# A fused embedding, quantized-attention and expert kernel on one core: V's way back, its rounding, and what stands ahead of three meetings

## The chip, the cores and the metric

The kernel runs on one core of one Trainium2 chip. The metric is the device time of one execution in microseconds (us), as the median of several runs.

## The reference

The reference embeds 64 images (36 patches each) and 64 texts (32 tokens each) to 192 features, gives them one layer of attention whose numbers are quantized, and then a layer of experts. Cut to the attention:

```python
y = x @ fq_weight(w_qkv).T + b_qkv          # x: 64 sequences of 68 rows, 192 wide
y, _ = fq_act(y)                            # scale from min and max over all of y, round to 8 bits
q, k, v = split(y)                          # 12 heads of 16
attn = einsum('bhnd,bhmd->bhnm', q, k) * hd ** -0.5
attn, s_attn = fq_act(attn)                 # scale from min and max over all scores
attn = int_log_softmax(attn, s_attn)        # integer softmax, powers of two
o = einsum('bhnm,bhmd->bhnd', attn, v)
o, _ = fq_act(o)                            # again min and max over everything
o, _ = fq_act(o @ fq_weight(w_proj).T + b_proj)
```

Each `fq_act` needs the extremes of a whole tensor before its first value can be rounded. So the program has stretches, and between them everything meets.

## The kernel before, in words

Every engine has a hand-written instruction stream. Semaphores order them, and `barrier` (L120) is a meeting of all five: each engine drains, counts `all_engines_done` up, and waits for five times the number of the meeting.

**Projections.** A loop over steps `s` makes, in each of 16 of its steps, one unit of Q, K and V. ScalarE moves Q and K from PSUM to SBUF. For V the vector engine (`scale_v`, L1306) scales PSUM into `vst`, which has two buffers by the unit's parity, and SyncE (`store_v`, L591) stores it to `v_rows` in DRAM, in the order sequence position, sequence, feature. `scale_v` of a unit waits (L1309) until the stores of the unit two before it have landed. `load_v` (L603) brings V back with all 68 positions of a run of sequences on 68 partitions: 51 KB a sequence. The list `V_LOADS` (L218) holds step, unit waited for, first and last sequence. All of this is on SyncE's one queue, in program order: in step 26 the loads of sequences 32 to 47 and 0 to 5, then the stores of units 14 and 7, after step 27 those of unit 15, then (L631) the load of 48 to 63.

**First meeting, then the first pass.** For each of 8 chunks `c` of 8 sequences ScalarE adds a magic number to Q and K (`to_halves`, L916), the vector engine rounds and clamps them (`to_whole`, L1390), and GpSimd spreads the last four positions' queries over heads (L753 to L762). SyncE loads sequences to the lower partitions (`load_four`, L640; `load_seqs`, L635), the tensor engine makes scores (`first_scores`), and the vector engine takes their row maxima and minima (`extremes`, L1407). After the last chunk ScalarE adds the magic number to all of V (`vt`, L940), and the vector engine rounds it to `VQ`:

```python
dve.wait_ge(sem("v_added"), 2)
ts(VQ, vt, s1(Q_CAPM, N), H16 + 512.0, ALU.min, ALU.subtract)
```

Then the vector engine reduces the extremes to one column each (L1434 to L1438), GpSimd reduces over the partitions (`reduce_pair`, L731; L764), and the vector engine makes some 45 scalars from the result (L1441 to L1491) and, in L1492 to L1495, constants for the output's bias (`bmask`, `vrow`, `bprow`).

**Second meeting, then the second pass.** It computes the scores again, two sequences a group, 32 groups: loads (`load_two`, L649), scores (`second_scores`, L1997), `distances` on the vector engine (L1505), remainders, logarithms, probabilities and the sum over V. GpSimd clears `stv` first (L774), and SyncE waits for that before its first load. `spread_v` (L655) copies `VQ` to `stv`. In its last step SyncE also issues `load_rest` (L662): the residual rows `hf` and the experts' weights `wsplit`.

**Third meeting**, then the output's extremes over the partitions, the projection of the output, and the experts.

Of the kernel before, what the change touches and what calls it, by code (L numbers as in the profile page):

```python
# [12 lines left out]
ALU = mybir.AluOpType  # L13
# [5 lines left out]
P = 128  # L19
B = 64  # L20
# [70 lines left out]
def program(nc, x, x_txt, tok_W, tok_b, tok_pos, embed, W1, b1, W2, b2, w_qkv, b_qkv, w_proj, b_proj,  # L91
            w_fc_sh, w_proj_sh, w1, w2, router_w, balance_bias, ident_c, headmask_c, select_c, lower_c, out):
    ctx = ExitStack()
    with ctx:
# [24 lines left out]

        def barrier(eng, name):  # L120

            n = barriers.get(name, 0) + 1
            barriers[name] = n
            eng.drain().then_inc(sem("all_engines_done"), 1)
            eng.wait_ge(sem("all_engines_done"), 5 * n)

# [90 lines left out]
        UNIT_ORDER = [UNITS_AT[k] for k in sorted(UNITS_AT)]  # L217
        V_LOADS = [(20, 11, 24, 32), (24, 12, 6, 24), (26, 6, 32, 48), (26, 6, 0, 6), (None, 15, 48, B)]  # L218
        LN_TILES = [(0, 16), (16, 22), (22, 28), (28, 34), (34, 37), (37, 40)]
# [297 lines left out]
        def _(sp):  # L517
# [91 lines left out]
            for s in range(STEPS + 1):  # L609
                if s in (5, 11):  # L610
                    sp.wait_ge(sem("by_patch"), s + 1)
                    load_images(2 + s // 6)
                for at, unit, first, end in V_LOADS:
                    if s == at:
                        if end == 48:
                            for a in range(2):
                                sp.wait_ge(sem(f"w_stored{a}"), 16 * sum(WCH_DMAS[a::2]))
                        if first == 0:
                            sp.wait_ge(sem("h_out"), 16 + 4 * GRID)
                        load_v(first, end, UNIT_ORDER.index(unit) if unit < 15 else 15)  # L620
                if s - 2 in WSTEP:
                    store_split(WSTEP.index(s - 2))
                if s in (7, 13, 19, 25):
                    store_image(s // 6 - 1)
                if s - 1 in UNITS_AT:
                    store_v(UNIT_ORDER.index(UNITS_AT[s - 1]))
            sp.wait_ge(sem("t_stored"), 16 * 16)
            for a in range(2):
                sp.wait_ge(sem(f"h_stored{a}"), 32)
            sp.wait_ge(sem("qkv_extremes"), 16)  # L630
            load_v(48, B, 15)  # L631
            barrier(sp, "sp")


# [13 lines left out]

            def load_two(g, par, half):  # L649
                wait(sp, "scored", 32 + g - 1)  # L650
                load_seqs(par, bass.ds(g * 2, 2), 2)

            pipeline(sp, [(load_four, 0)], 16)
            barrier(sp, "sp")
            def spread_v(g, par, half):  # L655
                wait(sp, "o_summed", g - 1)
                for b in range(2):
                    for a in range(2):
                        sp.dma_start(stv[:, par, b, a].rearrange("p (j h d) -> p j h d", h=2, d=HD)[:, :, a, :],  # L659
                                     VQ[:, bass.ds(g * 2 + b, 1), :].rearrange("p o (j h d) -> p (o j) h d", h=2, d=HD)[:, :, a, :]).then_inc(sem(f"v_spread{par}"), 16)  # L660

            def load_rest(g, par, half):  # L662

                if not (isinstance(g, int) and g == 31):
                    return
                for k in range(2):
# [3 lines left out]

            sp.wait_ge(sem("v_cleared"), 1)
            pipeline(sp, [(load_two, 0), (spread_v, 4), (load_rest, 4)], 32)
            barrier(sp, "sp")

# [43 lines left out]
        def _(pool):  # L718
# [34 lines left out]
            for c in range(8):  # L753
# [8 lines left out]
                last.then_inc(sem("qk_chunk"), 1)  # L762

            reduce_pair(A_MX, "a_minmax")  # L764
            barrier(pool, "pool")
# [38 lines left out]
        def _(act):  # L804
# [127 lines left out]
            for c in range(8):  # L932
                to_halves(c)

            act.wait_ge(sem("qk_whole"), 8)
            act.wait_ge(sem("qk_chunk"), 8)
            act.wait_ge(sem("v_in"), 16 * len(V_LOADS))
            for n in range(2):
# [182 lines left out]
        def _(dve):  # L1121
# [283 lines left out]


            def extremes(c):  # L1407
                for i in range(4):
# [17 lines left out]
            for c in range(9):  # L1426
                if c < 8:
                    to_whole(c)
                if c >= 1:
                    extremes(c - 1)  # L1430
            dve.wait_ge(sem("v_added"), 2)
            ts(VQ, vt, s1(Q_CAPM, N), H16 + 512.0, ALU.min, ALU.subtract)
            dve.wait_ge(sem("extremes"), 32)
# [57 lines left out]
            ch(dve.memset(s1(A_PB), 128.0 * (127.0 + 1.0 + H16) + 64.0))  # L1491
            for k, (lo, hi) in enumerate(((C1, C1 + 3), (C1 + 1, P), (C1 + 2, P))):  # L1492
                ch(dve.tensor_reduce(bmask[:, k:k + 1], ident[:, lo:hi], X, ALU.add, negate=k > 0))
            ch(dve.reciprocal(vrow, prow))
            ch(tt(bprow, bprow, vrow, ALU.mult))  # L1495
            barrier(dve, "dve")
# [345 lines left out]
        def _(pe):  # L1842
# [148 lines left out]
            def first_scores(g, par, half):  # L1991
                pe.wait_ge(sem(f"st_qk{par}"), (half + 1) * 48)
                for k in range(2):
                    wait(pe, "extremes", g * 2 + k - 1)
                    scores(g * 2 + k, 4 * k, par, 2 * k, 2)

            def second_scores(g, par, half):  # L1997
                pe.wait_ge(sem(f"st_qk{par}"), (8 + half + 1) * 48)
                wait(pe, "dist", g)
                scores(g, 0, par, 0, 1)  # L2000

            pipeline(pe, [(first_scores, 0)], 16)
            barrier(pe, "pe")

# [218 lines left out]
```

## Time and profile before

| | |
|---|---|
| time, median of 3 runs | 942.96 us (940.64 to 943.77) |
| the profiled execution | 945.13 us, span 943.2 us |
| TensorE's mean granted clock in it | 0.709 of full speed |
| busy: tensor, vector, scalar, GpSimd | 604.6, 709.8, 515.3, 252.1 us |
| HBM read and written | 45.62 and 31.85 MB, 82 GB/s over the span |
| chain that ended last, by engine | vector 28%, tensor 24%, issue 17%, SyncE's queue 16%, scalar 9% |

The profiled execution is one run of its own, 2.2 us above the median. The busy times overlap. The chain is followed back from the last instruction, at each step to what released it; its share by engine says on whom the end hung, and "issue" is time in which nothing recorded was waited for. Where a row names an engine with a q (SPq), it is the engine's queue, issuing.

### The profile page before, as it was taken

Reading aid. Unit: us, or ns where it says so; the run is one execution under the profiler, and the core shown is the slowest. Engines: PE = TensorE matmul, PEld = TensorE weight load, DVE = VectorE, ACT = ScalarE, POOL = GpSimd, SP = SyncE. Lnnn points to the kernel's source line nnn. Section 1 sums busy time; section 2 is a strip of 40 time slices with the busy share of each in tenths; the row PEclk is TensorE's granted clock in tenths of the full one; section 3 lists DMA queues with packets and bytes.
Section 4 is the critical chain, followed back from the end, with each engine's and each line's share of the span. In section 5 each row is a group of like instructions: output and inputs, shape, how many; then the busy total and the mean of one; then the engine's idle time right before and its main releaser. Section 6 shows DMA issues by size and latency. Waiting matters only on the chain.

```text
span 943.2 us, 19819 instructions
## 1 busy us (share of the span) xinstructions
PE 604.6 (64%) x6474; PEld 451.9 (48%) x6474; DVE 709.8 (75%) x1831; ACT 515.3 (55%) x951; POOL 252.1 (27%) x245
## 2 busy tenths in 40 slices
PE   3589889898406667058888888341222349999970
PEld 2589768776204334024555555331112237777760
DVE  2535668777548999789999999987776788667783
ACT  3122268766345424048888888454554226888840
POOL 2022111120011221012222222110355750036575
PEclk9999789999755555555565555555555569999985
DMA  7974024443222221022222222451011241467753
GB/s 172 258 202 120 18 54 131 109 119 120 96 66 82 68 68 51 9 47 33 43 43 43 43 43 37 106 220 59 33 55 58 77 147 51 140 188 218 226 168 113
DMA packets 151481, 92.77 MB, mean 98 GB/s; under 512 B 88828, under 2 KB 143684, under 8 KB 151084
## 3 DMA queue, kind: packets, MB, share of 16 engines
q1 hardware_dynamic: 143560, 72.28, 29.3%
q0 software_dynamic: 7856, 19.68, 7.2%
q8 instruction: 34, 0.56, 0.3%
q14 instruction: 31, 0.25, 0.1%
HBM read 45.62 MB, written 31.85 MB: 82 GB/s over the span
## 4 chain that ended last, share of the span: by engine, by line
DVE 28%; PE 24%; issue 17%; SPq 16%; ACT 9%; DMA 3%; POOL 2%; POOLq 0%; DVEq 0%; ACTq 0%
PE ps L1844 19%; SPq L659 8%; ACT R L806 5%; ACT R L809 3%; DVE M L1413 3%; DVE M L1414 3%; SPq L637 2%; POOL R L799 2%; SPq L636 2%; SPq L638 2%; DVE R L1403 2%; DVE R L1801 1%; PE ps L2018 1%; PE ps L2114 1%; PE ps L1869 1%
## 5 line engine op out<-in xcount | busy, mean ns | idle before, releaser
L1844 PE MATMUL ps<-R 128*128 128x256 f16 (+9 forms) x2064 | 310.2, 303 | 53.0 <-DVE R L1801 16.1
L1844 PEld LDWEIGHTS ps<-R 128*128 128x128 f16 (+5 forms) x2064 | 221.6, 129 | 113.3 <-issue 59.1
L806 ACT ACTIVATE R<-ps 128x768 f16<-128x768 f16 (+7 forms) x257 | 159.8, 649 | 93.5 <-PE ps L2018 18.9
L1844 PE MATMUL ps<-M 32*128 32x68 bf16 (+4 forms) x1196 | 100.6, 242 | 117.5 <-DMA M<-R 67.2
L1844 PEld LDWEIGHTS ps<-M 32*128 32x128 bf16 (+3 forms) x1196 | 64.9, 115 | 168.9 <-issue 66.5
L809 ACT ACTIVATE R<-R,sc 128x512 f16<-128x512 f32 (+7 forms) x107 | 83.6, 838 | 105.6 <-DVE R L1403 40.1
L799 POOL DMA_INDIRECT R<-y_by_tile,M x68 | 66.7, 981 | 98.0 <-DMA y_by_tile<-R 79.4
L771 POOL TENSOR_TENSOR R<-R,M 128x884 f32<-128x884 f32 x32 | 53.2, 1664 | 145.5 <-ACT M L958 145.5
L790 POOL DMA_INDIRECT x_by_expert<-R,M x68 | 67.2, 989 | 60.3 <-DVEq L1707 40.5
L806 ACT ACTIVATE R<-R 128x512 f16<-128x512 f32 (+4 forms) x121 | 64.1, 549 | 35.3 <-DVE R L1801 34.5
L2018 PE MATMUL ps<-ident_b,R 128*68 128x128 bf16 x416 | 53.8, 298 | 25.3 <-ACT R L806 23.9
L1844 PE MATMUL ps<-M,R 128*128 128x8 f16 (+3 forms) x358 | 38.7, 242 | 30.5 <-DVE R L1603 21.9
L2018 PEld LDWEIGHTS ps<-ident_b,R 128*68 128x68 bf16 x416 | 39.6, 160 | 33.0 <-ACT R L806 29.4
L2077 PE MATMUL ps<-ident_f,R 128*128 128x128 f16 x102 | 14.0, 309 | 60.4 <-DVE R L1652 60.4
L1806 DVE TENSOR_TENSOR R<-R 128x256 f16<-128x256 f32 x58 | 24.6, 425 | 36.5 <-ACT R L806 36.5
L1844 PE MATMUL ps<-R,M 68*32 68x4 bf16 (+3 forms) x1680 | 46.7, 208 | 3.7 <-DVE R L1314 2.5
L949 ACT ACTIVATE ps<-ps,sc 128x512 f32<-128x512 f32 x64 | 37.2, 603 | 18.2 <-PE ps L1844 17.2
L1511 DVE SCALAR_TENSOR_TENSOR R<-ps,sc,M 128x544 f16<-128x544 f32 x64 | 42.5, 706 | 6.2 <-PE ps L1844 5.6
L1844 PEld LDWEIGHTS ps<-M,R 128*128 128x128 f16 (+2 forms) x358 | 25.9, 119 | 41.2 <-issue 14.8
L741 POOL COPY R<-R 96x768 f32<-96x768 f32 x24 | 20.5, 863 | 91.0 <-PE ps L1906 91.0
L1413 DVE TENSOR_REDUCE M<-ps 128x8 f32<-128x544 f32 x64 | 41.3, 645 | 4.1 <-PE ps L1844 3.9
L1844 PEld LDWEIGHTS ps<-R,M 68*32 68x32 bf16 (+1 forms) x1680 | 36.2, 111 | 11.9 <-issue 5.0
(293 smaller groups left out, 1050.2 us busy)
## 6 DMA issues: line engine op xcount, KB each, us to landing
R<-x_by_expert SPq DMA_DIRECT2D x41, 192.0 KB, 2.6
y_by_tile<-R SPq DMA_DIRECT2D x41, 192.0 KB, 2.3
R<-in_x_dram SPq DMA_DIRECT2D x12, 576.0 KB, 9.0
M<-R SPq DMA_DIRECT2D x16, 260.0 KB, 2.3
M<-R SPq DMA_DIRECT2D x32, 130.0 KB, 2.0
R<-w_split SPq DMA_DIRECT2D x1, 4032.0 KB, 23.1
R<-h_rows SPq DMA_DIRECT2D x1, 3264.0 KB, 14.3
out_dram<-R SPq DMA_DIRECT2D x17, 192.0 KB
```

What stands on the lines that cost most here:

```text
L659: sp.dma_start(stv[:, par, b, a].rearrange("p (j h d) -> p j h d", h=2, d=HD)[:, :, a, :], VQ[:, bass.ds(g * 2 + b, 1), :].rearrange("p o ...
L771: pool.tensor_tensor(L[par], L[par], S[:, par, 1, :].unsqueeze(2).to_broadcast([P, SLOTS, N]), ALU.subtract).then_inc(sem("relative"), 1)
L790: pool.indirect_dma_start(xg, bass.IndirectOffsetOnAxis(ap=slot[:, n, k:k + 1], axis=0), rows2[:, n, :], None).then_inc(sem("scattered"), 16)
L799: pool.indirect_dma_start(gb[:, i % 4, j, k, :], None, yg[0:TILE * ready, :], bass.IndirectOffsetOnAxis(ap=y_slot[:, 2 * i + j, k:k + 1], ...
L806: return act.activation(out_, in_, ACT.Copy)
L809: return act.activation(out_, in_, ACT.Identity, scale=scale, bias=bias)
L949: act.activation(rem[:, cols], rem[:, cols], ACT.Square, bias=s1(A_BH)).then_inc(sem("sq"), 1)
L1413: dve.tensor_reduce(rowmax[:, g:g + 1, s0:s0 + 2 * k].rearrange("p o (a s) -> p (o a) s", a=2), sv, X, ALU.max)
L1414: last = dve.tensor_reduce(gmin[:, g * 2 + part:g * 2 + part + 1], sv, mybir.AxisListType.XYZ, ALU.min)
L1511: last = dve.scalar_tensor_tensor(D[:, s0:s0 + 2 * k, :].rearrange("p (a s) k -> p a s k", a=2), score_part(0, part), s1(A_NKK), m.unsquee ...
L1844: return pe.matmul(o, a, b, start=start, stop=stop, skip_group_check=True)
L2018: last = pe.transpose(pPT[:, i, :], slots(Pb[par])[:, at, :], ident_b[:, :])
```

## The change

1. The loads of V on SyncE's queue: steps 20 and 24 keep theirs, cut into pieces of 4 and of 6 sequences. The loads of step 26 and the last one go. In their place ScalarE issues ten loads of 2 or 4 sequences (`V_LATE`) after chunks 1 to 6 of the first pass. Before the first meeting SyncE waits until V and the split weights are stored.
2. GpSimd rounds V to `VQ`, after its last chunk and before the all-reduce of the extremes. The first `spread_v` waits for it (`v_whole`).
3. The constants of the output are made between `to_whole(1)` and `extremes(0)`.
4. `barrier` can take work that an engine issues between counting itself in and waiting. At the second meeting SyncE loads the sequences of groups 0 and 1 there, and the tensor engine makes group 0's scores; the loops leave them out. At the third meeting SyncE issues `load_rest` there.

```diff
-        def barrier(eng, name):
+        def barrier(eng, name, ahead=None):
             n = barriers.get(name, 0) + 1
             barriers[name] = n
             eng.drain().then_inc(sem("all_engines_done"), 1)
+            if ahead:
+                ahead()
             eng.wait_ge(sem("all_engines_done"), 5 * n)
...
-        V_LOADS = [(20, 11, 24, 32), (24, 12, 6, 24), (26, 6, 32, 48), (26, 6, 0, 6), (None, 15, 48, B)]
+        V_LOADS = [(20, 11, 24, 28), (20, 11, 28, 32), (24, 12, 6, 12), (24, 12, 12, 18), (24, 12, 18, 24)]
+        V_LATE = [(1, 0, 4), (1, 4, 6), (2, 32, 36), (2, 36, 40), (3, 40, 44), (3, 44, 48), (4, 48, 52), (4, 52, 56), (5, 56, 60), (6, 60, B)]
...
-            sp.wait_ge(sem("qkv_extremes"), 16)
-            load_v(48, B, 15)
+                sp.wait_ge(sem(f"v_saved{a}"), v_stores(16 + a))
+                sp.wait_ge(sem(f"w_stored{a}"), 16 * sum(WCH_DMAS[a::2]))
             barrier(sp, "sp")
...
+            def load_ahead():
+                for g in range(2):
+                    wait(sp, "scored", 32 + g - 1)
+                    load_seqs(g, slice(g * 2, g * 2 + 2), 2)
+
             pipeline(sp, [(load_four, 0)], 16)
-            barrier(sp, "sp")
+            barrier(sp, "sp", load_ahead)
             def spread_v(g, par, half):
+                if isinstance(g, int) and g == 0:
+                    sp.wait_ge(sem("v_whole"), 1)
...
-            pipeline(sp, [(load_two, 0), (spread_v, 4), (load_rest, 4)], 32)
-            barrier(sp, "sp")
+            pipeline(sp, [(load_two, 0), (spread_v, 4)], 32)
+            barrier(sp, "sp", load_rest)
...
+            pool.wait_ge(sem("v_added"), 2)
+            pool.tensor_scalar(VQ, vt, sc[0:N, Q_CAPM:Q_CAPM + 1], H16 + 512.0, ALU.min, ALU.subtract).then_inc(sem("v_whole"), 1)
             reduce_pair(A_MX, "a_minmax")
             barrier(pool, "pool")
...
             for c in range(8):
                 to_halves(c)
+                for at, first, end in V_LATE:
+                    if c == at:
+                        act.dma_start(yv[:, first:end, :], v_dram[:, first:end, :]).then_inc(sem("v_in"), 16)
...
                 if c < 8:
                     to_whole(c)
+                if c == 1:
+                    output_constants()
                 if c >= 1:
                     extremes(c - 1)
-            dve.wait_ge(sem("v_added"), 2)
-            ts(VQ, vt, s1(Q_CAPM, N), H16 + 512.0, ALU.min, ALU.subtract)
             dve.wait_ge(sem("extremes"), 32)
...
+            def scores_ahead():
+                pe.wait_ge(sem("st_qk0"), 9 * 48)
+                pe.wait_ge(sem("extremes"), 31)
+                scores(0, 0, 0, 0, 1)
...
             pipeline(pe, [(first_scores, 0)], 16)
-            barrier(pe, "pe")
+            barrier(pe, "pe", scores_ahead)
```

SyncE's queue in the last steps of the projections, before. L607 is a load of V, L600 and L596 are stores of V for image and text units, L588 stores residual rows:

```order
L596 DMA v_rows<-R 4x32x192 [waits v_scaled]
L596 DMA v_rows<-R 4x32x192
L607 DMA R<-v_rows 68x3072 [waits v_saved0,v_saved1,w_stored1,w_stored0]
L607 DMA R<-v_rows 68x1152 [waits v_saved1,v_saved0,h_out]
L600 DMA v_rows<-R 16x6x192 [waits v_scaled]
L600 DMA v_rows<-R 16x6x192 x2
```

And the same place now:

```order
L599 DMA v_rows<-R 4x32x192 [waits v_scaled]
L599 DMA v_rows<-R 4x32x192
L603 DMA v_rows<-R 16x6x192 [waits v_scaled]
L603 DMA v_rows<-R 16x6x192 x2
L599 DMA v_rows<-R 4x32x192 [waits v_scaled]
```

The two loads between the stores of unit 6 and those of unit 14 are gone from this queue.

GpSimd at the end of the first pass, before. The ISA row with operands is the all-reduce, the one without is a configuration of the engine:

```order
L758 TENSOR_TENSOR R<-R,headmask 64x8x64 [waits scored]
L733 ISA
L733 ISA sc<-sc 128x2 [waits a_minmax]
L774 MEMSET M 68x1536 [waits all_engines_done]
L771 ISA
```

And now:

```order
L763 TENSOR_TENSOR R<-R,headmask 64x8x64 [waits scored]
L770 TENSOR_SCALAR R<-R,sc 68x12288 [waits v_added]
L738 ISA
L738 ISA sc<-sc 128x2 [waits a_minmax]
L781 MEMSET M 68x1536 [waits all_engines_done]
```

The rounding stands between the last product and the configuration, so that both it and the all-reduce come behind it.

## Rows read from the trace of the kernel before

**Rows 1.** The page, first part: engine, busy us, share of span, instructions.
```profile
PE 604.6 (64%) x6474; PEld 451.9 (48%) x6474; DVE 709.8 (75%) x1831; ACT 515.3 (55%) x951; POOL 252.1 (27%) x245
```
**Rows 2.** The waits from 215 to 271 us: total, times, longest.
```profile
DVE R L1314 <- DMA v_rows<-R: 12.5, 1, 12.5
```
**Rows 3.** The timeline of SyncE's queue, from 240 us: start, us, what, issues.
```profile
245.66 0.63 SPq L607 DMA_DIRECT2D R<-v_rows  x2
246.34 1.85 SPq L600 DMA_DIRECT2D v_rows<-R  x3
248.94 8.52 SPq L596 DMA_DIRECT2D v_rows<-R  x2
```
**Rows 4.** Busy time by window: us, PE, PEld, DVE, ACT, POOL, clock, DMA share, GB/s.
```profile
252.00:263.00 11.00, 0.00 (x0) 0.00 (x0) 0.00 (x0) 0.00 (x0) 0.00 (x0) 0.60 0.25 82
```
**Rows 5.** The timeline of vector and tensor engine around the wait.
```profile
250.97 0.28 PE L1844 MATMUL ps<-R 3*96 3x192 bf16 x1
263.80 0.55 DVE L1314 CUSTOM_DVE_ANT_1 R<-ps,M 96x384 f32<-96x384 f32 x1 [12.49 <-DMA v_rows<-R]
```
**Rows 6.** The timeline at the end of the first pass.
```profile
360.83 10.91 ACT L809 ACTIVATE R<-R,sc 68x6144 f16<-68x6144 f32 x2 [19.65 <-DVE R L1403]
...
378.88 3.42 DVE L1432 TENSOR_SCALAR R<-R,sc 68x12288 bf16<-68x12288 f16 x1
...
383.64 0.38 POOL L733 PARTITION_ALL_REDUCE sc<-sc  x1 [23.01 <-DVEq L1438]
```
**Rows 7.** GpSimd's elementwise work: one timeline row, then groups (busy us, mean ns).
```profile
96.59 2.41 POOL L741 COPY R<-R 96x768 f32<-96x768 f32 x3
...
L758 POOL TENSOR_TENSOR R<-R,headmask 64x512 bf16<-64x512 f16 x8 | 8.5, 1058 | 8.2 <-PE ps L1844 7.6
...
L774 POOL MEMSET M<- 68x1536 bf16 x1 | 1.4, 1375 | 12.3 <-DVEq L124 12.3
...
L758 POOL TENSOR_TENSOR R<-R,headmask 128x512 bf16<-128x512 f16 x8 | 11.0, 1381 | 64.4 <-DVE R L1396 53.6 <-issue 10.9
```
**Rows 8.** GpSimd's configurations (ns, first and last start) and what followed two of them.
```profile
L733 POOLq MODIFY_POOL_CONFIG  x4: 1/6/11, 360.8 to 596.9; - x4
...
L758 POOLq MODIFY_POOL_CONFIG  x2: 7/9/11, 270.1 to 270.2; - x2
...
279.40 3.07 POOL L758 TENSOR_TENSOR R<-R,headmask 128x512 bf16<-128x512 f16 x3 [10.88 <-issue]
...
L729 POOLq MODIFY_POOL_CONFIG  x2: 32/32/32, 88.9 to 88.9; - x2
...
96.33 0.38 POOL L729 PARTITION_ALL_REDUCE sc<-sc  x1 [7.55 <-DVEq L1214]
```
**Rows 9.** The timeline of the output's constants, and of the first extremes.
```profile
393.77 0.66 DVE L1493 TENSOR_REDUCE M<-ident 128x1 f32<-128x3 f32 x3
...
395.85 0.36 DVE L1495 TENSOR_TENSOR M<-M 128x192 f32<-128x192 f32 x1
...
287.04 0.72 DVE L1413 TENSOR_REDUCE M<-ps 128x8 f32<-128x544 f32 x1 [3.90 <-PE ps L1844]
```
**Rows 10.** The timeline around the second meeting.
```profile
374.42 1.95 PE L1844 MATMUL ps<-M 32*128 32x68 bf16 x20 [0.29 <-DVE M L1414]
...
398.22 0.11 DVE L1569 MEMSET M<- 128x64 f32 x1
...
402.88 1.33 DVE L1511 SCALAR_TENSOR_TENSOR R<-ps,sc,M 128x544 f16<-128x544 f32 x2 [4.55 <-PE ps L1844]
```
**Rows 11.** The timeline around the third meeting.
```profile
604.93 8.73 SPq L669 DMA_DIRECT2D R<-w_split  x1
...
612.18 0.17 DVE L1577 TENSOR_SCALAR sc<-sc 128x2 f32<-128x2 f32 x1
...
613.97 0.38 POOL L733 PARTITION_ALL_REDUCE sc<-sc  x1 [17.50 <-SPq L124]
```
**Rows 12.** The waits of the tensor engine from 271 to 380 us.
```profile
PE ps L1844 <- DMA M<-R: 35.4, 2, 33.8
```

More of the change, by code:

```diff
@@ L614, in _ @@
                     if s == at:
[L615 to L620, printed above, removed]
+                        load_v(first, end, UNIT_ORDER.index(unit))
                 if s - 2 in WSTEP:
@@ L649, in load_two @@
             def load_two(g, par, half):
+                if isinstance(g, int) and g < 2:
+                    return
                 wait(sp, "scored", 32 + g - 1)
                 load_seqs(par, bass.ds(g * 2, 2), 2)
+            def load_ahead():
+                for g in range(2):
+                    wait(sp, "scored", 32 + g - 1)
+                    load_seqs(g, slice(g * 2, g * 2 + 2), 2)
             pipeline(sp, [(load_four, 0)], 16)
-            barrier(sp, "sp")
+            barrier(sp, "sp", load_ahead)
             def spread_v(g, par, half):
+                if isinstance(g, int) and g == 0:
+                    sp.wait_ge(sem("v_whole"), 1)
                 wait(sp, "o_summed", g - 1)
@@ L660, in spread_v, with load_rest @@
                                      VQ[:, bass.ds(g * 2 + b, 1), :].rearrange("p o (j h d) -> p (o j) h d", h=2, d=HD)[:, :, a, :]).then_inc(sem(f"v_spread{par}"), 16)
-            def load_rest(g, par, half):
-                if not (isinstance(g, int) and g == 31):
-                    return
+            def load_rest():
                 for k in range(2):
@@ L933, in _ @@
                 to_halves(c)
+                for at, first, end in V_LATE:
+                    if c == at:
+                        act.dma_start(yv[:, first:end, :], v_dram[:, first:end, :]).then_inc(sem("v_in"), 16)
             act.wait_ge(sem("qk_whole"), 8)
             act.wait_ge(sem("qk_chunk"), 8)
-            act.wait_ge(sem("v_in"), 16 * len(V_LOADS))
+            act.wait_ge(sem("v_in"), 16 * len(V_LOADS + V_LATE))
             for n in range(2):
@@ L1404, in to_whole, with output_constants @@
                 last.then_inc(sem("qk_whole"), 1)
+            def output_constants():
+                for k, (lo, hi) in enumerate(((C1, C1 + 3), (C1 + 1, P), (C1 + 2, P))):
+                    ch(dve.tensor_reduce(bmask[:, k:k + 1], ident[:, lo:hi], X, ALU.add, negate=k > 0))
+                ch(dve.reciprocal(vrow, prow))
+                ch(tt(bprow, bprow, vrow, ALU.mult))
             def extremes(c):
@@ L1491, in _ @@
             ch(dve.memset(s1(A_PB), 128.0 * (127.0 + 1.0 + H16) + 64.0))
[L1492 to L1495, printed above, removed]
             barrier(dve, "dve")
@@ L1995, in first_scores @@
                     scores(g * 2 + k, 4 * k, par, 2 * k, 2)
+            def scores_ahead():
+                pe.wait_ge(sem("st_qk0"), 9 * 48)
+                pe.wait_ge(sem("extremes"), 31)
+                scores(0, 0, 0, 0, 1)
             def second_scores(g, par, half):
+                if isinstance(g, int) and g == 0:
+                    return
                 pe.wait_ge(sem(f"st_qk{par}"), (8 + half + 1) * 48)
```

## The prediction

> **What bounds the kernel now.** I read the page first: vector engine busy 75% of the span, tensor engine 64%, both far from full [rows 1]. So no engine bounds the whole, and what an edit is worth has to be read at its place. I went to the waits, then to timeline and chain around the three meetings of all engines (`barrier`). They show four stretches in which the chain of waits runs through idle time or side work.
>
> First, the last projections. The vector engine has one wait of 12.5 us for a DMA that writes `v_rows` [rows 2]. SyncE's queue tells why: at 245.66 it issues two loads of V (sequences 32 to 47 and 0 to 5, 1122 KB), at 246.34 the three stores of unit 14, and the next stores take 8.52 us to issue [rows 3]. In between the DMA engines are busy a quarter, at 82 GB/s, and nothing else runs [rows 4]. 1122 KB at 82 GB/s are 14.0 us, so these loads fill the queue until about 260, and the stores behind them land late. `scale_v` of the last unit rewrites their buffer: the vector engine goes on at 263.80 after 12.49 us of idling, since 251.3, and the last matmul of the unit had ended at 251.25 [rows 5].
>
> Second, the end of the first pass. ScalarE adds the magic number to V from 360.83 to 371.74, the vector engine rounds V for 3.42 us from 378.88, and GpSimd's all-reduce, which the scalars wait for, starts at 383.64 [rows 6]. Third, from 393.77 to 396.21 the vector engine makes constants of the output ahead of the second meeting [rows 9], and then idles 4.55 us for the first loads and scores of the second pass [rows 10]. Fourth, at the third meeting everyone waits for SyncE, which needs 8.73 us to issue one load [rows 11].
>
> **The change part by part**, on the profiled execution's clock (945.13 us, 2.2 above the median of 942.96; I carry the difference over to the median).
>
> *V loads off the busy queue: -12.4.* The two loads of step 26 and the one of 48 to 63 leave SyncE; step 20's and step 24's stay, in pieces, the bytes unchanged, in a place where the vector engine shows no wait for a DMA now. So the stores of unit 14 are issued by 248.2 at the head of the queue. Vector engine and tensor engine are both ready at 251.3, so all 12.49 us go unless the stores need more than 3 us to land. Next late would be the last matmul, at no cost. The waits for all saved V, which SyncE now makes before the meeting, replace those that its last load made: nothing.
>
> *Rounding on GpSimd: +8.4 net, the 3.42 us saved on the vector engine included.* The vector engine loses 3.42 us, and its chain to the all-reduce (1.4 us) would be through at about 379.9 + 0.2. But the rounding stands on GpSimd's queue ahead of the all-reduce. It waits for ScalarE's second half, so it starts at 371.8. No row shows this instruction on GpSimd. By the nearest that reads and writes with one input, three copies of 768 elements in 2.41 us, 12288 elements take 12.85 us; the memset of 1536 in 1.375 us gives 11.0; the 512-element products with two inputs give 25.4 us (64 partitions) and 33.1 (128, beside the vector engine's work) [rows 7]. I take the copy, as one input stands nearest: end at 384.6. The Trainium skill, "GPSIMD Engine Reference", § 4.1, calls one-input work on GpSimd roughly line-rate and two-input work about 2x slower than VectorE; its § 3.1 gives 1.03 cycles at 1.2 GHz for a simple body, as an estimate 10.5 us, which would make the sum 2.3 us better.
>
> Then comes what the diff doesn't say. In the order of instructions GpSimd has an ISA row between its last product and the all-reduce, and the trace names it MODIFY_POOL_CONFIG. It ran at 360.8, straight after the last product, and was long over when the all-reduce's data came. The new rounding is ahead of it, so it now runs at 384.6 with the all-reduce waiting behind. Its price: after the pair at 270.1 the first product started at 279.40 after 10.88 us of "issue", 9.2 us behind the config. After the pair at 88.9 the all-reduce could start at 96.33: at most 7.4 us, as it waited for data [rows 8]. For the all-reduce I take 7.4, the row of the same operation; bounds 0 (no row shows a wait in this direction) and 9.2. The all-reduce starts at 392.0 instead of 383.64: +8.4. The Trainium skill, same page, § 2.1, puts the first call after such a config at about 6 us (5.95); with that the sum would be 1.4 us better. The rule speaks against this change, and is my forecast's mechanism rather than a rival's.
>
> *Constants to where the vector engine idles: -2.45.* Their 2.45 us go from 393.77. Their new place is behind `to_whole(1)`, where the engine idled 3.90 us until 287.04 for the first scores [rows 9]. That covers 2.45; without the cover they would cost what they save.
>
> *First loads and scores ahead of the meeting: -4.55.* SyncE's two waits for scores are met when the tensor engine ends its first pass at 376.37; the issue of both groups, six in all, and their landing have until then 10 us and more before the meeting. What stands behind the wait is SyncE's arrival at the meeting, also early enough, and nobody else. The tensor engine scores group 0 while the scalars are made. After the meeting only the clamping of the row maxima remains, over at 398.33 against 402.88 now [rows 10]. The second group's scores wait for the first distances as before. GpSimd's clearing of `stv` only gates loads of group 2.
>
> *SyncE meets before its long load: -1.4.* The vector engine is through at 612.33, the all-reduce runs at 613.97 for SyncE's sake [rows 11]. With 0.2 us of handover it starts at 612.5. The load itself is not issued later.
>
> *Ten loads on ScalarE's queue: +1.0.* ScalarE idles in the first pass, so the issues cost nothing there. But the first two pieces (306 KB, 3.8 us at 82 GB/s) go out at 281, just as the first sequences are loaded, for which the tensor engine has its wait of 33.8 us [rows 12]. Bounds: 0, and 3.8 if the sequences' packets come behind all of them; I take 1, as the tensor engine's loads are already issued in part when the pieces start to move. Behind it the first pass shows one more wait of the tensor engine for a load, 1.6 us, 35.4 less 33.8; the other eight pieces I cost at nothing, on the cover of the vector engine's own work, and each us by which a load came later than that cover would count.
>
> Sum: -12.4 + 8.4 - 2.45 - 4.55 - 1.4 + 1.0 = -11.4. 945.13 gives 933.7; on the median 931.5.
>
> **Rivals.**
> *The config costs nothing where it stands* (chance 0.20). For it: no row shows a reload delaying an all-reduce. Against: the 9.2 us at 270.1 stood on the path. The all-reduce follows the rounding at 384.8: +1.1 instead of +8.4, 924.3; with the memset's rate and no collision of loads 921.4.
> *GpSimd rounds at the pace of its products* (0.24 in three parts). For it: those rows have the same types in and out. Against: two inputs instead of one. The time moves by each us of it. Above 12.85 + 11.4 = 24.3 us (1.98 ns an element) the change is slower than before. At the 64-partition row, 25.4 us: 944.1. At the 128-partition row, 33.1 us: 951.8, the case on the other side. Slower by over 0.3% starts at 2.2 ns an element. Between 1.2 and 1.8 ns: 933 to 940. I give 0.08 to each part.
> *The stores stay late* (0.04): step 24's pieces hold them as those of step 26 did. The rows show no such wait at step 24 now. Then nothing of the 12.4 comes: 943.9.
> The forecast has 0.52.
>
> **How the numbers follow.** A measurement tells about 0.3%, 2.8 us, from no change. Faster: 0.52 + 0.20 + 0.08 = 0.80. Same: the middle part of the pace and late stores, 0.12. Slower: 0.08. The range goes down to the first rival's best, 921.5, and up to 940, the end of the pace still faster; what lies outside holds 0.20.
>
> **What would show it.** The wait for `v_rows` gone and no idle time over 1 us before the last `scale_v`. One GpSimd TENSOR_SCALAR of 68x12288 at 11 to 14 us, then 6 to 9 us of nothing before the all-reduce, both on the chain of waits, and the vector engine idle for some 12 us there. No idle time for `scored` at the start of the second pass. The third all-reduce released by the vector engine, not by SyncE. I would be wrong if the all-reduce followed the rounding within 1 us, if the rounding took over 18 us, or if the vector engine waited for a DMA before 252.

## The result, and the profile after

| | before | after |
|---|---|---|
| time, median | 943.37 us (4 runs, 940.64 to 947.03) | 964.94 us (4 runs, 960.04 to 970.26) |
| ratio, with its 95% interval | 1 | 1.0227 (1.0161 to 1.0293) |
| profiled execution, its span | 945.13, 943.2 us | 966.23, 964.3 us |
| mean granted clock | 0.709 | 0.693 |

The change is slower by 21.6 us; a gain of 11.4 was forecast. The two traces can be laid beside each other at moments that both have. Each line is the time from one moment to the next; the sum is the difference of the spans.

| stretch | before | after | change | forecast |
|---|---|---|---|---|
| start to the first meeting's all-reduce | 268.15 | 254.97 | -13.2 | -12.4 |
| to the first column of the extremes (L1434; now L1450) | 110.73 | 118.37 | +7.6 | +1.0 |
| to the second meeting's all-reduce | 4.76 | 40.71 | +35.9 | +8.4 |
| to the first distances (L1511; now L1523) | 19.24 | 12.24 | -7.0 | -7.0 |
| to the third meeting's all-reduce | 211.09 | 209.73 | -1.4 | -1.4 |
| to the end | 329.2 | 328.3 | -1 | 0 |

(The second line's moment before is the rounding's start of [rows 6], which stood where L1450 now does.) Two forecasts hold to the tenth and the first within 0.8; the two lines far off lie in the first pass and at its end. The lower mean clock asks for no term of its own: the last three lines, over half of the tensor engine's busy time, come out as forecast or 1 us better.

The page, first part and the groups of GpSimd (line, engine, operation, out<-in, count | busy us, mean ns | idle time before and its releaser), of the changed kernel:

```profile
PE 605.6 (63%) x6474; PEld 454.6 (47%) x6474; DVE 704.8 (73%) x1830; ACT 515.1 (53%) x951; POOL 292.2 (30%) x246
...
PE 29%; DVE 28%; issue 15%; ACT 12%; POOL 7%; DMA 6%; SPq 2%; ACTq 1%; DVEq 0%; POOLq 0%
...
L770 POOL TENSOR_SCALAR R<-R,sc 68x12288 bf16<-68x12288 f16 x1 | 41.6, 41647 | 11.2 <-ACT R L816 11.2
```

Against [rows 1], GpSimd is busy 40.1 us more with one instruction more, and the vector engine 5 us less. In the chain that ended last (the second line) SyncE's queue fell from 16% to 2%, while GpSimd rose from 2% to 7% and the DMA engines from 3% to 6%. The engine whose share of busy time is the smallest now bounds a place.

The timeline of the changed kernel at the end of the first pass (start us, us, engine, line, operation, [idle before <-releaser]):

```profile
355.29 10.91 ACT L816 ACTIVATE R<-R,sc 68x6144 f16<-68x6144 f32 x2 [16.70 <-DVE R L1413]
...
366.30 41.65 POOL L770 TENSOR_SCALAR R<-R,sc 68x12288 bf16<-68x12288 f16 x1 [11.21 <-ACT R L816]
...
373.34 0.62 DVE L1450 TENSOR_REDUCE sc<-M 128x1 f32<-128x448 f32 x1
...
414.05 0.37 POOL L738 PARTITION_ALL_REDUCE sc<-sc  x1 [6.10 <-issue]
...
414.45 0.16 DVE L1457 TENSOR_TENSOR sc<-sc 128x1 f32<-128x1 f32 x1 [39.86 <-POOL sc L738]
```

This answers to [rows 6]. The vector engine is through at 374.6 and idles 39.86 us. GpSimd rounds for 41.65 us what the vector engine rounded in 3.42, and the all-reduce comes 6.10 us behind it. The chain of waits over this stretch says the same from the other side, and shows where the 6.10 us lie:

```profile
366.30 41.65 POOL R L770
407.95 0.32 POOLq L124
408.30 5.75 issue
414.05 0.38 POOL sc L738
```

After 0.32 us of the queue's own work come 5.75 us in which GpSimd waits for nothing. GpSimd's configurations in the list of instructions by line (least, middle and longest ns, first and last start) now begin at 408.3, where [rows 8] have 360.8:

```profile
L738 POOLq MODIFY_POOL_CONFIG  x4: 11/11/11, 408.3 to 620.3; - x4
```

The end of the projections, SyncE's queue and the vector engine, answers to [rows 3] and [rows 5]:

```profile
244.24 1.85 SPq L603 DMA_DIRECT2D v_rows<-R  x3
248.35 1.17 SPq L599 DMA_DIRECT2D v_rows<-R  x2
...
250.62 0.54 DVE L1324 CUSTOM_DVE_ANT_1 R<-ps,M 96x384 f32<-96x384 f32 x1
```

No bracket of idle time stands behind the last row: the 12.49 us are gone. The first row is the three stores of unit 14, which that instruction waits for; the two of unit 7 behind them take 1.17 us to issue instead of 8.52.

The first pass is the other surprise. Waits of the changed kernel from 255 to 370 us (total, times, longest), and the tensor engine's timeline there:

```profile
PE ps L1856 <- DMA M<-R: 44.2, 6, 21.8
...
DVE M L1429 <- PE ps L1856: 12.7, 5, 3.7
```

```profile
272.49 3.84 PE L1856 MATMUL ps<-M 32*128 32x68 bf16 x40 [21.82 <-DMA M<-R]
...
287.87 3.85 PE L1856 MATMUL ps<-M 32*128 32x68 bf16 x40 [6.72 <-DMA M<-R]
...
302.78 3.84 PE L1856 MATMUL ps<-M 32*128 32x68 bf16 x40 [6.33 <-DMA M<-R]
...
315.68 3.84 PE L1856 MATMUL ps<-M 32*128 32x68 bf16 x40 [4.32 <-DMA M<-R]
...
328.47 3.84 PE L1856 MATMUL ps<-M 32*128 32x68 bf16 x40 [4.20 <-DMA M<-R]
```

Before, there were two such waits, the first of 33.8 us and one of 1.6 [rows 12]. Now there are six, four of them of 4 to 7 us, and behind five of them the vector engine waits too, 12.7 us in all instead of 3.9. What was late is in the chain of waits: the landings of the sequence loads, one before each of those matmuls.

```profile
267.14 5.21 DMA M<-R
...
279.11 8.61 DMA M<-R
...
294.47 8.17 DMA M<-R
...
309.38 6.16 DMA M<-R
...
322.28 6.05 DMA M<-R
```

In the kernel before the one landing in that chain took 2.00 us. What shares the DMA engines with them is ScalarE's pieces of V. Busy time by window (columns as in [rows 4]) between the sequence loads' issue and landing:

```profile
281.70:287.80 6.10, 0.00 (x0) 0.00 (x0) 4.45 (x10) 0.89 (x2) 1.49 (x1) 0.50 0.43 118
```

The second and third meetings answer to [rows 10] and [rows 11]:

```profile
371.85 1.19 PE L1856 MATMUL ps<-M 32*128 32x68 bf16 x16 [1.01 <-DMA M<-R]
...
628.74 8.72 SPq L674 DMA_DIRECT2D R<-w_split  x1
...
635.57 0.17 DVE L1589 TENSOR_SCALAR sc<-sc 128x2 f32<-128x2 f32 x1
...
636.02 0.37 POOL L738 PARTITION_ALL_REDUCE sc<-sc  x1 [16.16 <-DVEq L124]
```

The scores of the second pass's first group lie in the wait for the second meeting, and the third all-reduce is released by the vector engine 0.28 us after it is through, no longer by SyncE.

### The profile page after: what moved, and what is told of

Its sections match the earlier page's. It is cut to its first block, busy times and chain, and to the rows that moved or that the text cites. A ratio compares the mean times of both kernels' runs of the same rounds, so it can differ in the third digit from the quotient of the medians.

```text
span 964.3 us, 19831 instructions
## 1 busy us (share of the span) xinstructions
PE 605.6 (63%) x6474; PEld 454.6 (47%) x6474; DVE 704.8 (73%) x1830; ACT 515.1 (53%) x951; POOL 292.2 (30%) x246
## 3 DMA queue, kind: packets, MB, share of 16 engines
q10 hardware_dynamic: 720, 1.98, 0.8%
## 4 chain that ended last, share of the span: by engine, by line
PE 29%; DVE 28%; issue 15%; ACT 12%; POOL 7%; DMA 6%; SPq 2%; ACTq 1%; DVEq 0%; POOLq 0%
PE ps L1856 22%; ACT R L813 7%; POOL R L770 4%; DMA M<-R 4%; PE ps L2037 3%; ACT R L816 3%; DMA R<-in_L_txt_tok_embed_dram,R 2%; DVE M L1572 2%; DVE R L1813 2%; POOL R L806 2%; ACT ps L959 1%; DVE R L1523 1%; PE ps L2133 1%; DVE R L1548 1%; DVE M L1553 1%
## 5 line engine op out<-in xcount | busy, mean ns | idle before, releaser
L816 ACT ACTIVATE R<-R,sc 128x512 f16<-128x512 f32 (+7 forms) x107 | 83.6, 838 | 98.8 <-POOL R L763 40.1
L2037 PE MATMUL ps<-ident_b,R 128*68 128x128 bf16 x416 | 55.9, 307 | 24.5 <-ACT R L813 22.8
L2037 PEld LDWEIGHTS ps<-ident_b,R 128*68 128x68 bf16 x416 | 41.5, 166 | 32.2 <-ACT R L813 28.8
L1818 DVE TENSOR_TENSOR R<-R 128x256 f16<-128x256 f32 x58 | 24.6, 424 | 36.7 <-ACT R L813 36.7
L1429 DVE TENSOR_REDUCE M<-ps 128x8 f32<-128x544 f32 x64 | 41.2, 644 | 12.8 <-PE ps L1856 12.7
L770 POOL TENSOR_SCALAR R<-R,sc 68x12288 bf16<-68x12288 f16 x1 | 41.6, 41647 | 11.2 <-ACT R L816 11.2
L763 POOL TENSOR_TENSOR R<-R,headmask 128x512 bf16<-128x512 f16 (+1 forms) x16 | 19.4, 1216 | 80.4 <-DVE R L1406 42.5
```

The source lines that it names most:

```text
L770: pool.tensor_scalar(VQ, vt, sc[0:N, Q_CAPM:Q_CAPM + 1], H16 + 512.0, ALU.min, ALU.subtract).then_inc(sem("v_whole"), 1)
L816: return act.activation(out_, in_, ACT.Identity, scale=scale, bias=bias)
L1429: dve.tensor_reduce(rowmax[:, g:g + 1, s0:s0 + 2 * k].rearrange("p o (a s) -> p (o a) s", a=2), sv, X, ALU.max)
L1818: tt(hl[:, u % 4], hs[:, u % 2, 0], hh[:, u % 4, 0], ALU.subtract)
L2037: last = pe.transpose(pPT[:, i, :], slots(Pb[par])[:, at, :], ident_b[:, :])
```

## The experiments

Two theories had to be told apart at the rounding (its own pace, or what stands around it), two in the first pass (the loads of V, or a drift of the whole stretch), and the three terms that seemed right had to be shown to be right by themselves. Runs are compared with the kernel before on the same chip, and stretches of the traces with each other. The kernel before took 944.37 us beside the runs r5, r6, r7 and r12 and about 1025 us beside the others. In the traces of those others some 80 us more lie behind the third all-reduce (409.7 us in the run of the V loads alone, 329.2 in the kernel before), in the experts, where nothing was changed; of the kernel before itself there is no trace at 1025 us. I take it that ratios and stretches carry over; absolute times don't.

**1. The rounding back on the vector engine** (r1_round_dve), everything else as changed.

```diff
-            pool.wait_ge(sem("v_added"), 2)
-            pool.tensor_scalar(VQ, vt, sc[0:N, Q_CAPM:Q_CAPM + 1], H16 + 512.0, ALU.min, ALU.subtract).then_inc(sem("v_whole"), 1)
...
+            dve.wait_ge(sem("v_added"), 2)
+            ts(VQ, vt, s1(Q_CAPM, N), H16 + 512.0, ALU.min, ALU.subtract).then_inc(sem("v_whole"), 1)
```

> The changed kernel with one part undone: the vector engine rounds V again, 3.42 us behind its last extremes. Theory A (the loss is the rounding's place on GpSimd: 41.65 us of it, then 0.35 + 5.75 us of drain and config, all ahead of the all-reduce): the all-reduce runs at 373.3 + 3.4 + 1.4 + 0.2 = 378.3 instead of 414.05, the time falls by 35.7 us, from 966.2 to about 930.5, and the config is hidden again. Rival B (the collision of V's loads with the first pass, or something behind the second meeting, is most of the loss): it falls by less than 20 us, to 946 or more. In both the first pass keeps its five waits for late sequence loads.

1009.15 us (6 runs), ratio 0.9851 (0.9821 to 0.9881). The all-reduce stood 1 us ahead of where it was expected:

```profile
377.31 0.37 POOL L738 PARTITION_ALL_REDUCE sc<-sc  x1 [23.01 <-DVEq L1454]
```

So the whole change without its rounding on GpSimd is faster than before. The 36.7 us between 377.31 and 414.05 are what the rounding on GpSimd costs. The first pass stays long (118.96 us).

**2. Only the rounding on GpSimd, in the kernel before** (r2_pool_only).

```diff
-            dve.wait_ge(sem("v_added"), 2)
-            ts(VQ, vt, s1(Q_CAPM, N), H16 + 512.0, ALU.min, ALU.subtract)
...
+            pool.wait_ge(sem("v_added"), 2)
+            pool.tensor_scalar(VQ, vt, sc[0:N, Q_CAPM:Q_CAPM + 1], H16 + 512.0, ALU.min, ALU.subtract).then_inc(sem("v_whole"), 1)
             reduce_pair(A_MX, "a_minmax")
```

> The kernel before with that one part alone: GpSimd rounds V, everything else as before. Theory A: the rounding starts at 371.8, takes 41.65 us as in the changed kernel, config 6.1 us, the all-reduce at 419.5 instead of 383.64: 945.1 + 35.9 = 981 us. Rival C (the rounding was slow because of what the change put beside it, the last loads and scores ahead): it takes visibly less here, near the 12.85 us of the prediction, and the time is 950 to 955.

```profile
371.79 41.65 POOL L767 TENSOR_SCALAR R<-R,sc 68x12288 bf16<-68x12288 f16 x1 [11.21 <-ACT R L813]
419.43 0.37 POOL L735 PARTITION_ALL_REDUCE sc<-sc  x1 [5.99 <-issue]
```

One run, 1059.43 us, 34.3 above the median before. By the trace +35.8 (419.43 against 383.64). The same 41.65 us with none of the other edits: what the change put beside it has no part in it.

**3. What the pace hangs on.** Four kernels change only the instruction. r7_copy copies (clamp and subtraction are left out), r6_one_op subtracts only (the clamp is left out), r12_constants has both operations with a constant as the limit of the clamp (the limit is another), r5_half gives GpSimd sequences 0 to 31 and the vector engine the rest.

```diff
-            pool.tensor_scalar(VQ, vt, sc[0:N, Q_CAPM:Q_CAPM + 1], H16 + 512.0, ALU.min, ALU.subtract)
+            pool.tensor_copy(VQ, vt)                                                        # r7_copy
+            pool.tensor_scalar(VQ, vt, H16 + 512.0, None, ALU.subtract)                     # r6_one_op
+            pool.tensor_scalar(VQ, vt, H16 + 640.0, H16 + 512.0, ALU.min, ALU.subtract)     # r12_constants
```

> The changed kernel with GpSimd's rounding of V replaced by a plain copy of the same 12288 elements a partition, f16 to bf16 (clamp and subtraction left out). Theory G (GpSimd's pace hangs on the arithmetic: 3.39 ns an element for two operations, and the copy's pace that the prediction took would have been right for a copy): 12 to 14 us. Theory H (the 16-bit types or the sheer size make it slow): about 40 us.

> The changed kernel with the clamp left out of GpSimd's rounding: one operation, subtract a constant, same data. Theory G: half of the two operations' time or less, 13 to 21 us. Theory I (any TENSOR_SCALAR on GpSimd has this pace, whatever it does): 41.6 us.

> The changed kernel with the clamp's limit as a constant instead of a column of scalars (so V is clamped elsewhere): two operations, no pointer. Theory G: 41.6 us again. Theory J (the pointer operand is what costs): near the one-operation run.

> The changed kernel with sequences 0 to 31 rounded by GpSimd (6144 elements a partition) and 32 to 63 by the vector engine behind its last extremes. If the time goes by elements: 20.8 us on GpSimd, the all-reduce at 366.3 + 20.8 + 6.1 = 393.2 instead of 414.05, the time 20.8 us under the changed kernel's, about 945 on the chip of its profile. If there is a large fixed part: more than 25 us.

The timeline of GpSimd in each, in this order:

```profile
365.36 10.42 POOL L770 CAST R<-R 68x12288 bf16<-68x12288 f16 x1 [11.17 <-ACT R L816]
381.61 0.37 POOL L738 PARTITION_ALL_REDUCE sc<-sc  x1 [5.83 <-issue]
```
```profile
364.97 31.31 POOL L770 TENSOR_SCALAR R<-R 68x12288 bf16<-68x12288 f16 x1 [11.20 <-ACT R L816]
```
```profile
365.52 41.61 POOL L770 TENSOR_SCALAR R<-R 68x12288 bf16<-68x12288 f16 x1 [11.20 <-ACT R L816]
```
```profile
368.06 20.97 POOL L770 TENSOR_SCALAR R<-R,sc 68x6144 bf16<-68x6144 f16 x1 [11.21 <-ACT R L816]
395.01 0.37 POOL L738 PARTITION_ALL_REDUCE sc<-sc  x1 [5.99 <-issue]
```

And the vector engine's half in r5_half:

```profile
375.10 15.54 DVE L1450 TENSOR_SCALAR R<-R,sc 68x6144 bf16<-68x6144 f16 x1
```

| | us | ns an element | one run, us (before: 944.37) |
|---|---|---|---|
| copy | 10.42 | 0.85 | 939.54 |
| one operation | 31.31 | 2.55 | 957.32 |
| two operations, constants | 41.61 | 3.39 | 965.3 |
| two operations, limit from a pointer (as changed) | 41.65 | 3.39 | 966.23 |
| half the elements | 20.97 | 3.41 | 950.45 |

The pace hangs on what the instruction does: from the copy to one operation +1.70 ns, to two another +0.84. The pointer costs nothing, and half the elements cost half. The one-operation run fits neither theory named for it: 31.31 us, against 13 to 21 and against 41.6. The copy took less than the 12 to 14 us expected. A pace like the copy's, on which the forecast rested, is real for a copy, and the copy's run is the forecast's picture: all-reduce at 381.61, 5.83 us behind. Even so that run is only 4.8 us under the kernel before, one run each, where 11.4 had been forecast with a slower copy: its first pass, up to the first column of the extremes, takes 119.76 us instead of 110.73.

The run with half the elements came out at 950.45 us instead of about 945. Its rounding started 1.8 us later than expected, and 2.9 us more lie behind its third all-reduce than in the changed kernel. Its trace shows one thing more. The vector engine's half took 15.54 us, where all of V takes it 3.42 alone: it began at 375.10 beside GpSimd's instruction, which ended at 389.03, and ended 1.6 us after it, and half of 3.42 is 1.71. It looks as if it could hardly move until GpSimd was through; why, no run here isolates. The reductions of float32 from PSUM beside the same instruction kept their 0.57 and 0.71 us. So sharing this rounding between the two engines gains less than the sum of their paces would give.

The Trainium skill, "GPSIMD Engine Reference", § 3.1, has 1.03 cycles an element for a body with a k of at most 2 (read here as the number of operations), at 1.2 GHz as an estimate 10.5 us. The copy agrees; the two operations with one input take four times that. Its § 4.1 calls one-input work roughly line-rate against the vector engine: measured are 3.42 us there and 41.65 here, a factor of 12.

**4. The V loads alone, in the kernel before** (r11_v_only).

```diff
-        V_LOADS = [(20, 11, 24, 32), (24, 12, 6, 24), (26, 6, 32, 48), (26, 6, 0, 6), (None, 15, 48, B)]
+        V_LOADS = [(20, 11, 24, 28), (20, 11, 28, 32), (24, 12, 6, 12), (24, 12, 12, 18), (24, 12, 18, 24)]
+        V_LATE = [(1, 0, 4), (1, 4, 6), (2, 32, 36), (2, 36, 40), (3, 40, 44), (3, 44, 48), (4, 48, 52), (4, 52, 56), (5, 56, 60), (6, 60, B)]
...
                 to_halves(c)
+                for at, first, end in V_LATE:
+                    if c == at:
+                        act.dma_start(yv[:, first:end, :], v_dram[:, first:end, :]).then_inc(sem("v_in"), 16)
```

> The kernel before with the V loads of the change alone (five pieces in steps 20 and 24, ten on ScalarE's queue beside the first pass; rounding, constants and meetings as before). The prediction's -12.4 + 1.0 = -11.4 us against the theory now: the stall of 12.5 us goes, the first pass gives about 7 us of it back in five waits for late sequence loads, net -5 to -6 us, ratio about 0.994.

1018.95 us (12 runs) against 1024.74 (17): ratio 0.9948 (0.9917 to 0.9979), a gain of 5.8 us. The forecast's -12.4 + 1.0 would have been 0.988. The same waits are there as in the changed kernel:

```profile
PE ps L1843 <- DMA M<-R: 44.6, 5, 23.2
...
DVE M L1412 <- PE ps L1843: 16.2, 5, 7.2
```

The all-reduce comes at 379.25, 4.4 us before its old time. The first meeting's comes 13.2 us earlier, and from it to the rounding the first pass takes 119.49 us instead of 110.73: 8.8 us are given back there.

**5. The same late loads, each cut into rows 0 to 63 and 64 to 67** (r3_64_and_4), on top of experiment 1.

```diff
-                        act.dma_start(yv[:, first:end, :], v_dram[:, first:end, :]).then_inc(sem("v_in"), 16)
+                        for rows in (slice(0, 64), slice(64, N)):
+                            act.dma_start(yv[rows, first:end, :], v_dram[rows, first:end, :]).then_inc(sem("v_in"), 16)
```

> As r1_round_dve, and each of the ten late loads of V is cut into rows 0 to 63 and rows 64 to 67; bytes, queue and place unchanged. Theory D (a load of 68 rows runs on 4 of the 16 DMA engines, as the busy share of 0.25 says, and the sequence loads queue behind V on just those four): spread over more engines the pieces are over sooner, the five waits of the tensor engine for a load (6.7, 6.3, 4.3, 4.2, 0.8 us) shrink to under 2 us in all, and the time is 6 to 8 us under r1_round_dve, about 923. Rival E (the collision is one of bytes, or of two queues taking turns): no change, 930.

999.1 us (5 runs, 995.51 to 1000.44), ratio 0.975 (0.972 to 0.9779). The waits from 250 to 366 us, a window in which a piece moves, and the all-reduce:

```profile
PE ps L1857 <- DMA M<-R: 26.8, 5, 18.9
...
DVE M L1428 <- PE ps L1857: 0.5, 1, 0.5
```
```profile
271.00:276.00 5.00, 3.35 (x28) 2.11 (x27) 5.00 (x10) 4.99 (x8) 0.00 (x0) 0.50 0.73 170
```
```profile
363.05 0.38 POOL L738 PARTITION_ALL_REDUCE sc<-sc  x1 [23.01 <-DVEq L1455]
```

The landing of the sequence loads can be read directly. In the DMA issues of the first pass (KB each, median us to landing) the smallest of each three is, in the changed kernel and here:

```profile
M<-R SPq DMA_DIRECT2D x10, 34.0 KB, 6.0
...
M<-R SPq DMA_DIRECT2D x13, 34.0 KB, 2.5
```

The same row of the kernel before has 2.0. The same bytes on the same queue, twice as many loads, and the first pass takes 106.98 us from the all-reduce to the end of the extremes instead of 118.96 in experiment 1. The vector engine's waits fall from 13.3 to 0.5 us. With 68 rows a load of V moved at 82 GB/s with the DMA engines a quarter busy [rows 4]; with 64 rows the window shows 0.73 busy and 170 GB/s, sequence loads included; experiment 6 has a window without them. A quarter of 16 is what the Trainium skill, "DMA: Bandwidth & Descriptors", section "Why a DMA increments its semaphore by 16 and not by 1", would give: the engines used are the largest number up to 16 that divides the slowest dimension on both sides, 4 for 68 rows and 16 for 64. Shares and rates agree; no row here shows which engine carried what. The gain over experiment 1 is 10 us, where 6 to 8 were expected. This is the version to keep: 2.5% below the kernel before.

**6. No late loads in the first pass, but a burst ahead of it** (r8_burst), on top of experiment 1: `V_LATE` is empty, and SyncE issues three loads, each cut at row 64, before the first meeting.

```diff
+            sp.wait_ge(sem("qkv_extremes"), 16)
+            for first, end in ((0, 6), (32, 48), (48, B)):
+                for rows in (slice(0, 64), slice(64, N)):
+                    sp.dma_start(yv[rows, first:end, :], v_dram[rows, first:end, :]).then_inc(sem("v_in"), 16)
             barrier(sp, "sp")
```

> As r1_round_dve, but the late loads of V leave the first pass: SyncE issues them in one burst of three, each in rows 0 to 63 and 64 to 67, after the last unit's extremes and before the first meeting. The first pass then has no V load beside it unless the burst (1938 KB) lasts more than 8 us. Theory D: the first pass has no wait for a late load behind its first, -7.6 us, against a config that takes up to 2.6 us longer beside the loads (9.2 us beside one in the kernel before, 6.6 us without in the changed one): 923 to 926. Rival F (the waits in the first pass come from the shifted start, not from V's loads): they stay, 930 or more.

1007.45 us (5 runs), ratio 0.9818 (0.9786 to 0.9849). That is 1.7 us under experiment 1, within the spread of the two, where 4 to 8 us had been expected. Waits, GpSimd's first product and its configuration, and a window in which the burst alone moves:

```profile
PE ps L1860 <- DMA M<-R: 23.5, 1, 23.5
...
DVE M L1431 <- PE ps L1860: 3.0, 1, 3.0
```
```profile
268.51 3.31 POOL L767 TENSOR_TENSOR R<-R,headmask 128x512 bf16<-128x512 f16 x3 [13.01 <-issue]
...
L767 POOLq MODIFY_POOL_CONFIG  x2: 7/9/11, 257.1 to 257.1; - x2
```
```profile
257.10:262.80 5.70, 0.00 (x0) 0.00 (x0) 1.48 (x7) 4.29 (x8) 0.00 (x0) 0.50 0.97 223
```

Without loads beside it the first pass has one wait of the tensor engine, so the waits of the changed kernel are the late loads' doing and no drift. In the window the DMA engines are 0.97 busy at 223 GB/s, against 0.25 and 82 with 68 rows. But the burst stands beside the configuration ahead of the first product, and from the one to the other it is now 11.4 us (257.1 to 268.5) where the changed kernel has 6.6 (257.0 to 263.63). Up to 2.6 us more had been expected. The extremes' stretch is 113.8 us, between those of experiments 1 and 5. Spreading V in 64-row pieces beats the burst.

**7. The two terms of the second meeting, each undone** on top of experiment 1. r9_no_ahead puts the loads and scores back behind the meeting; r10_const_back puts the constants back behind the scalars.

```diff
-            barrier(sp, "sp", load_ahead)
+            barrier(sp, "sp")
...
-            barrier(pe, "pe", scores_ahead)
+            barrier(pe, "pe")
```
```diff
-                if c == 1:
-                    output_constants()
...
             ch(dve.memset(s1(A_PB), 128.0 * (127.0 + 1.0 + H16) + 64.0))
+            output_constants()
```

> As r1_round_dve, without the loads and scores ahead of the second meeting. The vector engine then idles again for the first scores behind the meeting, 4.5 us, and the time is 4.5 us over that kernel's. If the loads ahead had cost something elsewhere (they stand on SyncE's queue ahead of its wait), less than 4.

> As r1_round_dve, with the constants of the output back between the scalars and the second meeting: from the all-reduce to the first distances 2.45 us more, and the same first pass, as its first scores come late with or without them.

From the all-reduce to the first distances experiment 1 has 12.26 us. Without the work ahead it is 16.56 (+4.30):

```profile
381.48 0.38 POOL L736 PARTITION_ALL_REDUCE sc<-sc  x1 [23.01 <-DVEq L1452]
...
398.04 1.33 DVE L1521 SCALAR_TENSOR_TENSOR R<-ps,sc,M 128x544 f16<-128x544 f32 x2 [4.34 <-PE ps L1854]
```

With the constants back it is 14.72 (+2.46). Both are single runs, 1023.1 and 1018.7 us, and experiment 1's profiled execution took 1014.37. Of the first one's 8.7 us, 4.2 lie ahead of the all-reduce, though its edit comes behind it: its first pass takes 121.75 us up to the rounding, against 118.96 in experiment 1. In the second it takes 122.5, where the same had been expected; whether the constants have a part in that, one run can't tell. Only the stretch behind the all-reduce is evidence.

## Why the prediction was wrong

**The rounding: the term that failed.** "I take the copy, as one input stands nearest" is the step. It put 12.85 us where 41.65 stand, and that alone is 28.8 of the 33 us between forecast and result. The sum with 41.65 in the same place would have been +17.4 instead of -11.4, the right sign and four fifths of the size. The rows had a pointer to it: the products have the same types and do arithmetic, while the copy and the memset do none. The nearest row was sought by the number of inputs; by experiment 3 one operation on one input costs 2.55 ns an element, as much as the products on two (2.1 to 2.7), so in these rows arithmetic makes the difference, and the number of inputs makes little. Even the upper bound, 33.1 us, was 8.5 us short: a product has one operation, and the rounding two. The rival "GpSimd rounds at the pace of its products" had the right sign and half of the mechanism: it took the pace of rows that do arithmetic, but had no term for the second operation. Its worst part (951.8) came nearest, and it was given 0.24 in all. Its condition, slower from 1.98 ns an element, was met at 3.39. The rounding took over 18 us, as the prediction's own sign of being wrong had it. A small slip beside it: 1.8 ns an element are 22.1 us, which the forecast's sum makes 940.8 and not 940.

**The configuration: right.** It moved behind the rounding, with the all-reduce waiting. I took 7.4 us; what now lies between them measures 6.1. The rival that it costs nothing falls in all six kernels that have the rounding on GpSimd: 5.8 to 6.2 us of idle time each. The Trainium skill, "GPSIMD Engine Reference", § 2.1, has 5.95 us for a first call, and the changed kernel's row agrees with 5.75, where next to no load ran beside it. My 9.2 us from [rows 8] stood beside a load of 816 KB of V (DMA share 0.25). At that same place it is 6.6 us with a share of 0.01 and 11.4 beside the burst with 0.73, so the load's part is inferred from three values; no run varied it alone.

**The late loads: the second term that failed.** +1.0 was taken (bounds 0 and 3.8), +7.6 came, and that with 2.6 us won back because the configuration ahead of the first product no longer runs beside the long load (11.25 us from all-reduce to first product before, 8.66 now). The collision itself is some 10 to 11 us: 7.6 and 2.6, or 118.37 against 106.98 in experiment 5. The failed step is "the other eight pieces I cost at nothing, on the cover of the vector engine's own work". I had priced the first collision by its bytes and no other, though each chunk issues its pieces just when the next sequences are loaded, and the quarter-busy window of [rows 4] showed that such a load fills few of the engines for long. The text did say that every us past the cover would count.

**The stall: right.** -12.4 was forecast, and the stretch is 13.2 shorter; 0.7 of the rest is the vector engine arriving earlier, ready at 250.62 instead of 251.3. The stores of unit 14, issued from 244.24, had landed by then. But experiment 4 shows that the term and the late loads belong together: net they are worth 5.8 us, not 11.4.

**Constants, work ahead, SyncE before its load: right.** 7.0 us forecast and 7.0 measured, apart 2.46 and 4.30 by experiment 7 instead of 2.45 and 4.55. At the third meeting -1.4, and the release is the vector engine's as stated.

In sum, from the forecast's terms on the profile's clock: -11.4, +28.8 for the pace, -1.3 for the configuration, +6.6 for the late loads, -0.8 for the stall, and -1 behind the third meeting give +20.9; the spans differ by 21.1.

## What to carry to other kernels

An operation put on another engine is priced by a row with the same kind of work there, operation count included, and if none exists the range must reach past the worst of its neighbours, since a slow engine with the lowest share of busy time becomes the bound as soon as a meeting stands behind it. A load that keeps few DMA engines busy for long delays its neighbours (here 68 rows, with a share of 0.25); cut it at 64 rows before moving it beside anything urgent. Look at what a moved instruction displaces in its engine's order: here a configuration that had been free became 6 us of the path.

## What was not expected of the hardware

- GpSimd's elementwise work on 68x12288, float16 to bfloat16: 0.85 ns an element for a copy, 2.55 with one operation, 3.39 with two. The vector engine took 3.42 us for the two, 0.28 ns an element, but 15.54 us for half of the elements when GpSimd worked on the other half.
- The time from MODIFY_POOL_CONFIG to GpSimd's next instruction is longer beside a load: 5.75 us (all-reduce) and 6.6 (product) with next to none, 9.2 (product) beside a load of 816 KB, 11.4 (product) beside the burst.
- A load of 68 rows delays small loads of others that share the DMA engines: their landing on the chain went from 2.00 to between 5.2 and 8.6 us. With the same bytes in 64 and 4 rows the vector engine's waits shrank to 0.5 us.
- Beside seven of these runs the kernel before took 1025 us, beside the other four 944. The seven traces have their 80 us behind the third all-reduce. Why the experts' stretch is longer there stays open; it wasn't tried.
